# Ranking channels in eight steps beside the tiles of a GroupNorm and patch top-k kernel

## The reference, cut to what matters

```python
x                                   # (4, 256, 256, 256) float32: images, channels, height, width
xn = (x - mean) / sqrt(var + 1e-5)  # GroupNorm, 32 groups of 8 channels of one image
s = 0.5 * grad_mag(xn) + 0.5 * abs(xn)      # |left-right neighbour difference| + |up-down difference|
sp = s.reshape(4, 256, 8, 32, 8, 32).mean(axis=(3, 5)).reshape(4, 256, 64)   # 64 patches of 32 x 32
ranks = argsort(argsort(-sp, axis=1), axis=1)     # rank of each channel within its patch
mask = ranks < 128                                # the better half of the channels, patch by patch
out = x + xn * mask                               # xn only where the channel is kept in that patch
```

## Time and profile before

| what | us |
|---|---|
| median of the runs | 2195.79 |
| the profiled execution, its own time | 2193.39 |
| its span in the trace | 2192.2 |
| outside of the span | 1.2 |
| DVE busy | 1849.2 |
| PE, ACT, POOL busy | 1401.2, 1443.8, 1316.9 |

### The profile page before, as it was taken

One profiled execution on the slowest core, in us unless ns is written; L12 is line 12 of the kernel. 1 busy time (PEld: TensorE's weight loads), 2 busy tenths in 40 slices (PEclk: granted clock), 3 DMA queues, 4 the chain that ended last, 5 costly groups with the idle time before them and its releaser, 6 DMA issues.

```text
span 2192.2 us, 15457 instructions
## 1 busy us (share of the span) xinstructions
PE 1401.2 (64%) x3503; PEld 698.8 (32%) x3503; DVE 1849.2 (84%) x3133; ACT 1443.8 (66%) x2377; POOL 1316.9 (60%) x1052
## 2 busy tenths in 40 slices
PE   5877777767477766676577768775776868640000
PEld 2443333333233333333233333342333434320000
DVE  8999999979599899989779989989999999976000
ACT  4666666669387776778396777769767677741343
POOL 4533333357386666678376676777756667544476
PEclk9898888878788878897788879887888978875555
DMA  9999999659899999988989999946979997318887
GB/s 403 393 403 400 401 405 422 236 243 387 368 398 421 420 420 419 375 343 339 418 352 424 422 405 418 413 182 254 422 304 383 419 419 302 143 73 325 339 304 260
DMA packets 94556, 777.02 MB, mean 354 GB/s; under 512 B 17656, under 2 KB 17656, under 8 KB 76032
## 3 DMA queue, kind: packets, MB, share of 16 engines
q1 hardware_dynamic: 20736, 536.88, 59.0%
q0 software_dynamic: 73728, 239.17, 28.7%
HBM read 427.82 MB, written 402.65 MB: 379 GB/s over the span
## 4 chain that ended last, share of the span: by engine, by line
DVE 52%; issue 15%; POOL 14%; DMA 12%; PE 2%; ACT 2%; DVEq 2%; POOLq 1%; SPq 0%
DVE larger L719 20%; DVE stats L697 16%; DMA out_dram<-slots,rows 7%; POOL slots L357 4%; POOL out_dram L372 4%; DVE end_sums L743 3%; POOL place L320 3%; DVE sums L746 2%; DMA slots<-in_x_dram,rows 2%; DVEq L687 2%; DMA ring<-in_x_dram 2%; DVE scratch L834 1%; DVE largest L832 1%; DVE scratch L835 1%; DMA out_dram<-ring 1%
## 5 line engine op out<-in xcount | busy, mean ns | idle before, releaser
L537 PE MATMUL vertical<-ring,plus 128*128 128x512 f32 (+1 forms) x1280 | 711.3, 640 | 88.3 <-ACT vertical L659 87.5
L719 DVE SCALAR_TENSOR_TENSOR larger<-ring 128x960 bf16<-128x960 f32 x488 | 718.6, 1509 | 20.2
L539 PE MATMUL vertical<-ring,minus 128*128 128x512 f32 (+1 forms) x1280 | 679.1, 615 | 0.0
L697 DVE BATCH_NORM_STATS2 stats<-ring 128x6 f32<-128x512 f32 x1024 | 625.0, 678 | 15.5 <-DMA ring<-in_x_dram 12.0
L320 POOL TENSOR_TENSOR place<-ring 128x960 f32<-128x960 f32 x192 | 440.0, 2293 | 257.1 <-ACT place L653 227.6
L666 ACT ACTIVATE thrown<-ring,record 128x1024 bf16<-128x1024 f32 x512 | 581.9, 1136 | 3.3 <-DVE record L708 0.8
L659 ACT ACTIVATE vertical<-vertical 128x960 f32<-128x960 f32 x320 | 304.2, 951 | 365.4 <-PE vertical L539 364.8
L623 ACT ACTIVATE slots<-slots,offset,factor 128x1024 f32<-128x1024 f32 x256 | 309.6, 1229 | 327.5 <-DMA slots<-in_x_dram,rows 169.2
L357 POOL DMA_INDIRECT slots<-in_x_dram,rows x256 | 274.6, 1073 | 209.3 <-DMA out_dram<-slots,rows 100.7
L537 PEld LDWEIGHTS vertical<-ring,plus 128*128 128x128 f32 x1280 | 266.4, 216 | 353.7 <-issue 258.2
L539 PEld LDWEIGHTS vertical<-ring,minus 128*128 128x128 f32 x1280 | 268.6, 210 | 319.8 <-issue 319.8
(11 more groups left out here) (102 smaller groups left out, 969.4 us busy)
## 6 DMA issues: line engine op xcount, KB each, us to landing
ring<-in_x_dram SPq DMA_DIRECT2D x63, 4096.0 KB, 16.5
out_dram<-ring SPq DMA_DIRECT2D x51, 4096.0 KB, 27.9
out_dram<-ring SPq DMA_DIRECT2D x14, 2048.0 KB, 12.5
out_dram<-in_x_dram SPq DMA_DIRECT2D x12, 2048.0 KB, 56.7
ring<-in_x_dram SPq DMA_DIRECT2D x4, 1024.0 KB, 7.8
slots<-in_x_dram,rows POOLq DMA_INDIRECT x256
out_dram<-slots,rows POOLq DMA_INDIRECT x256
```

The lines of the kernel that those rows point to most:

```text
L537: nc.tensor.matmul(v[:, first:end], plus[:], xs[:, first + 2 * PATCH:end + 2 * PATCH], start=True, stop=False)
L539: done = nc.tensor.matmul(v[:, first:end], minus[:], xs[:, first:end], start=False, stop=True)
L697: nc.vector.bn_stats(stats[:, k, :], buffer[:, k * BN:(k + 1) * BN])
L719: nc.vector.scalar_tensor_tensor(out=larger[w % 2][:].rearrange("p (r c) -> p r c", r=PATCH), in0=xs[:, w, :, 2:], scalar=0.0, in1=xs[:, w ...
```

## The change

The ranking is spread. Scores are made tile by tile: each tile gets its own spread, variance and scale on POOL (ten small instructions, one column wide) and TensorE. From the ninth tile of an image (`FIRST_STEP` is 8) each new tile is followed by a *step*: two rounds over the channels seen so far pick the next 16 for each patch: of the first 16(t + 1) channels those come out that are among the 128 kept whatever the later tiles hold. A step makes two blocks. Blocks are gathered one a tile from the tenth tile after the image's first one (`LAG` is 10), so the gathers of an image begin inside it and ten blocks are left after the last tile. The last two tiles of every image are dense and ACT finishes them between the sums of the next tile. One of the eight across sums moves from DVE to TensorE and ACT. `finish_across` is gone: one `tensor_tensor` by weights and one reduce (`total`) put all eight kinds together. All stores are sent in the order of the tiles.

```diff
-DENSE_FROM = (LAST, LAST, LAST, TILES - RING)
+FIRST_STEP = (CHANNELS - KEPT) // TILE_CH      # 8
+STEPS = TILES - FIRST_STEP                     # 8
+DENSE_FROM = 14
+COLUMNS = STEPS * BANDS
+BLOCKS = COLUMNS // BLOCK                      # 16 an image
+STEP_BLOCKS = BANDS // BLOCK                   # 2
+LAG = FIRST_STEP + 2
-ORDER = "o0 a0 o1 v0 o2 a1 o3 p0 a2 v1 a3 p1 a4 v2 a5 a6 v3 p2 a7 v4".split()
+ORDER = "o0 a0 o1 v0 o2 a1 o3 p0 a2 v1 a3 a4 v2 a5 p1 a6 v3 a7 v4 p2 v5".split()
+ORDER_DENSE = ("o0 a0 o1 v0 o2 a1 o3 p0 a2 v1 a3 d0 d1 v2 d2 d3 a4 p1 d4 a5 v3 d5 d6 a6 d7 v4 a7 p2 v5"
+               .split())
...
         # POOL, for every tile
-                n = tile - TILES
-                if n >= 2:
-                    scatter_block(n - 2)
-                wait_loaded(pool, tile)
...
+                n = tile - LAG
+                wait_loaded(pool, tile)
+                partition_spread(tile)
+                difference(tile, 0)
+                if n >= 2:
+                    scatter_block(n - 2)
+                if n >= 0:
+                    gather_block(n)
+                scales(tile)
+                end_columns(tile)
+                difference(tile, 1)
+                columns_at_edge(tile)
+                difference(tile, 2)
...
-            for n in range(STREAMED, ALL_BLOCKS):
+            scatter_block(ALL_TILES - LAG - 2)
+            for n in range(ALL_TILES - LAG, ALL_BLOCKS):
                 gather_block(n)
-                if n >= STREAMED + 1:
-                    scatter_block(n - 1)
+                scatter_block(n - 1)
             scatter_block(ALL_BLOCKS - 1)
...
         # SP, for every tile
+                if not (dense(tile) or copied_tile(tile)):
+                    store_tile(tile)
...
+                if tile and dense(tile - 1):
+                    store_finished(tile - 1)
                 if RING <= tile + RING - 1 < ALL_TILES:
                     load_tile(tile + RING - 1)
...
         # TensorE, for every tile
+                wait_loaded(pe, tile)
+                variance(tile)
+                inner(tile, 0)
+                if tile:
+                    move_scores(tile - 1)
+                inner(tile, 1)
+                turn_if_step(tile - 1)
+                inner(tile, 2)
+                rows_at_edge(tile)
+                inner(tile, 3)
+                inner(tile, 4)
+                if tile + 1 < ALL_TILES:
                     mean(tile + 1)
+                inner(tile, 5)
...
         # VectorE
+            def total(tile):
+                wait_summed(dve, tile)
+                nc.vector.tensor_tensor(weighed[:], sums[tile % RING],
+                                        weights[:].unsqueeze(2).broadcast_to([PARTS, KINDS, COLS]), ALU.mult)
+                settle()
+                nc.vector.tensor_reduce(totals[:], weighed[:].rearrange("p k w -> p w k"), AX.X, ALU.add)
+            def pick(tile):
+                seen = left[:, 0:(t + 1) * TILE_CH]
+                for k in range(2):
+                    nc.vector.max(largest[:, k], seen)
+                    nc.vector.max_index(picked[:, 8 * k:8 * k + 8], largest[:, k], seen)
+                    nc.vector.match_replace(out=seen, in_to_replace=largest[:, k], in_values=seen, imm_value=-1.0)
...
+            def step(tile):
+                now, prev = tile < ALL_TILES, tile - 1
+                ranked = prev >= 0 and prev % TILES >= FIRST_STEP
+                if now:
+                    inner_across(tile, (0, 1))
...
+                if prev >= 0:
+                    total(prev)
+                if now:
+                    stable_variance(tile)
+                if prev >= 0:
+                    score(prev)
+                statistics(tile + 1, 0)
+                if prev >= 0:
+                    keep_scores(prev)
+                if ranked:
+                    pick(prev)
+                statistics(tile + 1, 1)
+                if ranked:
+                    choices(prev)
+                if now:
+                    inner_across(tile, (2, 3, 4))
+                    statistics(tile + 1, 2)
+                    end_columns(tile)
+                    statistics(tile + 1, 3)
+                    inner_across(tile, (5, 6))
+                    rows_at_edge(tile)
+                    minus_mean(tile + 1)
+                    columns_at_edge(tile)
```

More of the change, by code:

```diff
@@ L160, in groupnorm_patch_topk @@
[L160 to L170, removed]
@@ L355, in gather_block @@
                 for j in range(BLOCK):
-                    row = rows[image % 2][:, first + j:first + j + 1]
+                    row = rows[:, column(n, j):column(n, j) + 1]
                     nc.gpsimd.indirect_dma_start(slot(n, j), None, x_rows,
@@ L511, in mean, with variance @@
                     .then_inc(mean_ready, 1)
+            def variance(tile):
+                pe.wait_ge(spread_ready, tile + 1)
+                nc.tensor.matmul(var_bank, averager[:], spread[:], start=True, stop=True).then_inc(var_ready, 1)
             def rows_at_edge(tile):
@@ L577, in _, with turn_if_step @@
+                last.then_inc(turned, 1)
+            def turn_if_step(tile):
+                if tile >= 0 and tile % TILES >= FIRST_STEP:
+                    turn_order(tile)
             pe.wait_ge(constants, CONSTANTS)
@@ L723, in end_columns @@
             def end_columns(tile):
-                if across(tile):
-                    dve.wait_ge(ends_ready, sum(across(t) > 0 for t in range(tile + 1)))
-                    nc.vector.tensor_reduce(end_sums[:], ends[:], AX.XY, ALU.add)
+                dve.wait_ge(ends_ready, tile + 1)
+                nc.vector.tensor_reduce(sums[tile % RING][:, ENDS, 0:ACROSS], ends[:, 0:ACROSS], AX.XY, ALU.add)\
+                    .then_inc(ends_free, 1)
             def columns_at_edge(tile):
@@ new lines, in choices @@
+            def choices(tile):
+                image, t = tile // TILES, tile % TILES
+                s = t - FIRST_STEP
+                columns = slice(s * BANDS, (s + 1) * BANDS)
+                dve.wait_ge(turned, steps_until(tile))
+                if dense(tile):
+                    made = coef[:, tile % 2]
+                    shift = factors[:, image % 2, 1, t:t + 1]
+                    if dense_until(tile) > 2:
+                        dve.wait_ge(dense_finished, 2 * (dense_until(tile) - 2))
+                    nc.vector.tensor_scalar(made[:, 0], mask_bank, scale[:, tile % RING:tile % RING + 1], 1.0,
+                                            ALU.mult, ALU.add)
+                    nc.vector.tensor_scalar(made[:, 1], mask_bank, shift, None, ALU.mult).then_inc(coef_ready, 1)
+                last = (image - 1) * BLOCKS + (s + 1) * STEP_BLOCKS - 1
+                if last >= 0:
+                    for b in range(max(0, last - SETS + 1), last + 1):
+                        dve.wait_ge(scattered[b % SETS], 16 * BLOCK * (blocks_before(b) + 1))
+                nc.vector.tensor_copy(rows[:, columns], picked_bank).then_inc(rows_ready, 1)
```

652 lines of the change are left out of this document (238 added, 414 removed).

## The result

The changed kernel takes **2920.84 us** (median of four runs, 2920.31 to 2922.07), the kernel before 2193.69 beside it: a ratio of 1.331, 95% interval 1.325 to 1.336. Forecast were 2143 us and a range up to 2275, so it is slower by a third where 2.4% less was predicted. The profiled execution has a span of 2918.6 us.

The account below looks back on a forecast made before the run. DVE bounds the first image, DVE and DMA later ones, POOL's issues the end. Start, steps of 27.0, 31, 31.9 and 30.0 us, dense tiles and late loads reach 1972; plus 168 gives 2140, forecast 2143 us, range 2045 to 2275.

Parts of the forecast that it names:

- rival A: POOL becomes the pace, first drains after issues costing 2.5 us: two gaps 2290 us, chance 0.13; one 2183, chance 0.17.
- The "against" (no gap at L392): Evidence against POOL becoming the pace: L392, behind the drain after the power and 9 us later, shows no gap.
- idle time ahead of POOL's second small instruction: Sign that the forecast is wrong: idle time appearing on POOL ahead of its second small instruction.
- DVE waiting for `ends`: Sign that the forecast is wrong: DVE waits for `ends` in most unranked steps by more than 3 us.
- DMA 30.0: Unranked step with gather: load, store, gather and scatter are 12.6 MB, at 420 GB/s 30.0 us; 24 such steps.
- no gather, not ranked: Eight steps: 21.3 us of DVE work, 2.4, and collisions of 1.7 to 5; 27.0 us taken, as now.
- gather, ranked: 29 steps: DVE work 21.3 plus 5.6 for ranking, plus 5.0 waiting between DVE and POOL: 31.9 us, ends 30.7 and 36.6.
- The end: After tile 63's mean: scatter 54 issued at 61 us, remaining scatters and gathers 94, last wait 13: 168 us, bounds 150 and 190.
- the queue lags and catches up in ranked steps: Lower bound of 28.6 us for an unranked step with gather, from POOL's and DVE's work instead of DMA's 30.0.
- The mean of 4.9 us of mutual waiting: Waiting between DVE and POOL per tile, 311 us together in the kernel before, used for the ranked step with gather.
- the five terms up to the end of `end_columns`: POOL in an unranked step with gather: 1.9 + 2.2 + 11.2 + 2.4 + 1.5 = 19.4 us after the mean.
- Rival B: POOL keeps the way over four instructions, so ranked steps with gather take 36.6 us: 2279 us in all; chance 0.17.

Follow-up runs that it names:

- run 2: The changed kernel, drains kept, with a tile's scatter and gather issues moved behind the scales: 2377.94 us, a single execution.
- 3: The kernel before with one POOL drain added behind the gather issues of 42 tiles: 2781.53 us, a single execution, against 2198.78.
- 5: The changed kernel with POOL's drains replaced by semaphore waits, plus one drain a tile between scatter and gather issues: 2900.85 us, a single execution.
- 10: The changed kernel, drains kept, with SP's load of three tiles ahead held until the present tile's gather has landed: 2354.63 us, ratio 1.070.
- run 1: The changed kernel with POOL's drains replaced by waits on a semaphore of its own: 2335.31 us, ratio 1.059.
- run 7: The changed kernel with semaphore waits for POOL's drains, and SP's load of three tiles ahead held until the gather has landed: 2075.35 us, ratio 0.945.
- run 8: The changed kernel with semaphore waits for drains, ACT's four finished places later in its order, and SP's load held until the gather landed: 2063.84 us, ratio 0.942.
- the same hold: SP's load of three tiles ahead waits until the gather has landed; in the kernel before: 2164.01 us, ratio 0.983.

## Why the prediction was wrong, point by point

**The step that failed** is rival A, in its size and its mechanism. The prediction saw the first drain behind indirect issues, L383's 2.77 us, said "for nothing that the profile shows", and priced it at 2.5 us wherever it occurs, as a fixed sum; the forecast itself has no term for it. It is no fixed sum: the first drain behind issues lasts until they have landed, 18.3 us on average (986.7 / 54). The kernel before has drains only at an image's last tile, where one of the differences stands between the issues and the spread: the drain came 6 us after the last gather issue, and POOL's queue had moved its last packet 1.9 us before the drain began. The DMA view of the kernel before from 1919.1 to 1925 us:

```profile
DMA packets 0, 0.00 MB, mean 0 GB/s; under 512 B 0, under 2 KB 0, under 8 KB 0
```

So that row showed a drain with nothing left to land, and its 2.77 us are not a landing; what they are stays open (run 2 has 0.81 in that case). The change puts seven drains into every tile, the first one behind the issues 0.6 us after the last of them. The "against" (no gap at L392) was read wrongly: L392 and its like are free because the drain ahead of them has waited for everything; in the changed kernel no instruction behind a later drain waits more than 0.4 us. That the drain waits for the landing is what runs 2, 3, 5 and 10 show. A source for a better guess was in the earlier trace rows already, where ACT waits 17.90 us for a gather. A wait of that kind should have been priced with such a row. Two of the prediction's own signs of being wrong came true: idle time ahead of POOL's second small instruction (of the scales, not of the spread), and DVE waiting for `ends`.

**The second miss** was covered by the first: "DMA 30.0" was worked out as bytes by rate, and the earlier trace rows was read as that limit. The sum says nothing of the order inside a step. The gather shares by packets, not by bytes, which costs run 1 260 us (run 7 against it). The prediction took steps with a gather to be limited either by DVE and POOL or by the sum of bytes; a queue that lags and catches up stood there only as what makes a step shorter.

With both removed, the rest of the sum can be compared with run 7:

| step of the prediction | predicted | run 7 |
|---|---|---|
| no gather, not ranked (tiles 1 to 9) | 27.0 | 25.4 |
| gather, not ranked (tiles 34 to 40) | 30.0 | 30.0 |
| the same, tiles 50 to 57, of which 50 to 53 were copied and aren't stored | not told apart | 28.5 |
| gather, ranked (57 to 63) | 31.9 | 30.3 |
| the same with a dense tile | 35.9 | 34.1 |
| tile 63's mean | 1972 | 1896 |
| from there to the end | 168 | 167 |

- The end was right, and for its reason: 174 us after and 167 in run 7. In the changed kernel the scatter of block 54 is issued 61 us behind tile 63's mean, as predicted, and four issues take 5.2 us.
- The 30.0 of unranked steps with all four transfers agrees with run 7 but not with run 8, where the same six steps (tiles 34 to 40) take 28.6, the bound worked out for POOL and DVE. Its windows over these steps and over the ranked and dense ones behind them:

```profile
1018.00:1190.00 172.00, 149.46 (x384) 72.87 (x384) 143.64 (x249) 133.72 (x222) 141.54 (x150) 0.94 1.01 421
1210.00:1440.00 230.00, 194.03 (x501) 94.33 (x499) 207.02 (x428) 172.40 (x282) 179.06 (x181) 0.90 0.94 377
```

  172 us at 421 GB/s are 72.4 MB, where six tiles are 75.6 by the prediction's 12.6: the DMA engines are full and some 3 MB short, and have room (377 GB/s) for these in the steps that follow. This is the prediction's lower bound, "the queue lags and catches up in ranked steps"; bytes by rate bound a long stretch, not each step.
- Steps without gather and ranked ones are 1.6 to 1.8 us shorter. The mean of 4.9 us of mutual waiting was carried over from before, but less came: in run 7 the across sums have a mean of 1419 ns against a median of 1157, and `weighed` 1063 against 221 at its shortest: 448 x 0.262 + 64 x 0.842 = 171 us, 2.7 a tile.
- A slip without consequence: the five terms up to the end of `end_columns` add up to 19.2 us and not 19.4 (and eight issues of 1.3 are 10.4 and not 11.2). In run 7, at tile 40, it takes 20.1.
- In the changed kernel the waiting of L743 went on in the one instruction of the same kind that replaced it:

```profile
L669 DVE SCALAR_TENSOR_TENSOR larger<-ring 128x960 bf16<-128x960 f32 x448 | 626.8, 1441 | 16.3 <-issue 0.4
L649 DVE BATCH_NORM_STATS2 stats<-ring 128x6 f32<-128x512 f32 x1024 | 630.0, 677 | 9.3 <-DMA ring<-in_x_dram 9.2
...
L699 DVE TENSOR_TENSOR weighed<-sums,weights 128x64 f32<-128x64 f32 x64 | 125.0, 1954 | 31.0 <-ACT vertical L609 30.7
```

  The longest across sum is 3297 ns and the longest `weighed` 2250, 2.15 and 2.03 us over their shortest, about one `difference` of POOL (2.2). Rival B (POOL keeps the way over several instructions) didn't show. By the Trainium skill, "SBUF — State Buffer", section "Who interferes with whom", the instruction that issues first has the shared ports for its whole length and the other one blocks. A wait of at most one instruction's length agrees with that, where the 7.50 us of the earlier trace rows didn't.
- The power of one column takes 0.59 us (0.4 predicted), dense tiles 4 us each as predicted. The changed kernel's steps behind dense tiles reach 74.1 us, where run 7 stays at 34. These are the drain again and not late loads: in the two longest steps the wait ahead of L385 is 44.8 and 45.2 us, while DVE's statistics wait for loads for 9.2 us in the whole execution (L649 above).
- With both causes removed the change is worth more than the 2.4% forecast: the same hold gives 2164 us without the change and 2075 with it, 4.1%.

## What to carry to other kernels

An idle time ahead of an instruction behind a drain, on the engine that issues indirect DMAs, has to be priced by the landing of those DMAs, not by the small gap that one lucky place shows; look there whether the queue was still moving anything. Order the engine's own instructions by a semaphore instead. Beside a queue with 32 KB packets a queue whose packets had 3.5 KB got a tenth of the bytes, whatever its urgency: start the large transfers after the urgent small ones have landed, or cut them into pieces of about the small ones' size. And a bound of bytes by rate holds for a long stretch; it tells neither the length of each step in it nor who is served first.

## What the runs showed of the hardware

- A drain on POOL waits for the indirect DMAs, both directions, that POOL has issued: 24.73, 21.64 and 19.50 us in three kernels. It waits for POOL's own queue alone: POOL went on 0.6 to 1.2 us behind its queue's last packet in all 54 waits of the changed kernel, and in 21 waits of run 2 while SP's queue was still moving. With the queue empty, a drain behind earlier issues cost 0.81 us in run 2 (24 times).
- Two DMA queues with work are served packet by packet: 97 to 97 with 3.15 and 0.34 MB, 401 to 394 with 1.46 and 1.44 MB. Splitting into 4 KB hardly lowered the sum: 414 GB/s beside 428.
- A semaphore wait on POOL for its own last instruction costs nothing visible: in run 7 the small products of the scales, 0.19 us long, start every 0.27 us, with drains that have nothing to wait for every 0.34.
